# Attention scores from 64-row products on the two partition halves, without stacked copies

## What is computed

```
q = l2norm(x Wq) * q_scale            # (8 batches, 16 heads, 512, 64)
k = l2norm(x Wk) * k_scale
v = x Wv
attn = softmax(q k^T * 64**-0.5)      # 512 x 512 for each head
out  = (attn v) Wo + bo
x    = x + gate_a * out
x    = x + gate_b * moe(layernorm(x) * (1 + cb) + sb)
```

## Time and profile of the kernel before

| | |
|---|---|
| median of 3 runs | 1470.58 us (1469.07 to 1471.44) |
| span of the profiled execution | 1467.0 us |
| attention stage | from about 45 us to 1131 us |
| PE busy over the span | 1343.3 us (92%) |
| DVE, ACT, POOL busy over the span | 1103.4, 1058.0, 645.9 us |
| SBUF-to-SBUF copies into `stack` | 256 DMAs of 384 KB, 6.4 us from issue to landing |

### The profile page before, as it was taken

The page is one execution under the profiler, slowest core; times in us unless marked ns, Lnnn a source line. Parts: engine busy times, 40 slices in busy tenths (PEclk is TensorE's granted clock), DMA queues, the critical chain, the costliest instruction groups (busy, mean ns, idle before and its releaser), DMA issues. The chain is left out here.

```text
span 1467.0 us, 27427 instructions
## 1 busy us (share of the span) xinstructions
PE 1343.3 (92%) x7114; PEld 913.1 (62%) x7114; DVE 1103.4 (75%) x2179; ACT 1058.0 (72%) x2650; POOL 645.9 (44%) x1279
## 2 busy tenths in 40 slices
PE   4699999999999999999999999999998377899997
PEld 4566666666665666666566666666654255677775
DVE  4478768776886787688768876876874798588887
ACT  3577868876887687688768877876875366677776
POOL 2245435543534454344336433443433666344443
PEclk8799999999999999999999999999999599899999
DMA  5344334543334344333435433354334000534331
GB/s 126 87 106 111 87 87 93 120 95 85 89 88 99 80 111 106 88 87 87 98 82 113 100 90 87 87 118 100 86 87 115 1 0 0 119 88 98 89 91 39
DMA packets 90054, 129.05 MB, mean 88 GB/s; under 512 B 12816, under 2 KB 55320, under 8 KB 89880
## 3 DMA queue, kind: packets, MB, share of 16 engines
q1 hardware_dynamic: 88696, 126.67, 38.3%
q10 hardware_dynamic: 1184, 0.40, 0.1%
HBM read 24.16 MB, written 2.23 MB: 18 GB/s over the span
## 5 line engine op out<-in xcount | busy, mean ns | idle before, releaser
L814 DVE TENSOR_REDUCE neg_max<-bank 128x1 f32<-128x512 f32 x512 | 350.2, 684 | 219.1 <-PE bank L525 212.5
L687 ACT ACTIVATE probs<-bank,neg_max 128x512 f32<-128x512 f32 x512 | 354.1, 692 | 144.1 <-DVE neg_max L814 139.5
L534 PEld LDWEIGHTS bank<-ident,probs 128*128 128x128 f32 x2048 | 236.1, 141 | 243.2 <-issue 150.0
L534 PE MATMUL bank<-ident,probs 128*128 128x128 f32 x2048 | 322.7, 280 | 1.9 <-ACT probsT L695 1.9
L556 PE MATMUL bank<-probsT,v_tok 128*64 128x512 f32 x1024 | 275.7, 617 | 0.9 <-DVE probsT L821 0.9
L524 PE MATMUL bank<-operands 128*128 128x512 f32 x512 | 236.8, 462 | 30.9 <-DMA operands<-operands 14.6
L50 POOL TENSOR_TENSOR rn_t<-rn 128x16 f32<-128x16 f32 x192 | 43.0, 224 | 367.5 <-DVE rn L41 357.5
L525 PE MATMUL bank<-operands 128*128 128x512 f32 x512 | 203.9, 398 | 0.0
L821 DVE COPY probsT<-bank 128x512 f32<-128x512 f32 x256 | 173.7, 678 | 0.6 <-PE bank L534 0.6
L661 ACT ACTIVATE qk_tok<-bank 128x256 f32<-128x256 f32 x256 | 99.1, 387 | 97.2 <-PE bank L494 96.8
L695 ACT ACTIVATE probsT<-bank 128x512 f32<-128x512 f32 x256 | 153.6, 600 | 11.3
(11 more groups left out here) (214 smaller groups left out, 2609.0 us busy)
## 6 DMA issues: line engine op xcount, KB each, us to landing
operands<-operands SPq DMA_DIRECT2D x256, 384.0 KB, 6.4
probsT<-gate_scratch SPq DMA_DIRECT2D x64, 256.0 KB, 5.0
out<-x_all SPq DMA_DIRECT2D x8, 256.0 KB, 2.4
probsT<-in_L_ffn_fc_w SPq DMA_DIRECT2D x1, 1024.0 KB, 8.9
raw<-in_L_attn_Wq SPq DMA_DIRECT2D x1, 512.0 KB, 4.6
raw<-in_L_attn_Wk SPq DMA_DIRECT2D x1, 512.0 KB, 7.5
raw<-in_L_attn_Wv SPq DMA_DIRECT2D x1, 512.0 KB, 8.8
raw_o<-in_L_attn_Wo SPq DMA_DIRECT2D x1, 512.0 KB, 8.9
```

What stands on the lines that cost most here:

```text
L534: last = nc.tensor.transpose(T_BANK[i % 2][:, j * P:(j + 1) * P], probs[:, i % 4, j * P:(j + 1) * P], ident[:])
L687: nc.scalar.activation(probs[:, i % 4], S_BANK[i % 3][:], ACT.Exp, bias=neg_max[:, i:i + 1], accum_out=row_sum[:, hp % 2, i:i + 1]).then_i ...
L814: nc.vector.reduce_max(neg_max[:, i:i + 1], S_BANK[i % 3][:], AX.X, negate=True).then_inc(max_done, 1)
```

## The change

`stack`, the four DMAs and the semaphores `stack_a` and `stack_b` are gone. `parts` is kept twice, for even and odd units, in the same SBUF space. `scores` makes a pair of tiles at once, the same 128 queries of both heads. It issues six products of 64 rows, head 0's on partitions 0 to 63 and head 1's on 64 to 127, in turns, into two PSUM banks. So `slot` calls it at even steps only. A tile's number i now means token tile i // 2 and head i % 2, and the banks rotate over a whole batch (`s_bank`). `high_q`, which writes the parts of the next unit, waits for the score products of the unit that used the same half of `parts`, instead of for the DMAs.

```
-    def scores(u, hp, i):
-        g = S_TILES * u + i
-        if i == 0:
-            pe.wait_ge(stack_a, 32 * (u + 1))
-        if i == NT:
-            pe.wait_ge(stack_b, 32 * (u + 1))
-        after(pe, p_done, g - (2 if i >= 3 else 4 if i == 2 else 1))
-        head, t = i // NT, i % NT
-        st = stack[:, hp % 2, head]
-        q = st[:, ST_Q, t * P:(t + 1) * P]
-        nc.tensor.matmul(S_BANK[i % 3][:], q, st[:, ST_K], start=True, stop=False)
-        nc.tensor.matmul(S_BANK[i % 3][:], q, st[:, ST_KX], start=False, stop=True).then_inc(s_ready, 1)
+    def scores(u, hp, pair):
+        if pair == 0:
+            pe.wait_ge(kl_done, u + 1)
+        first = S_TILES * hp + 2 * pair
+        after(pe, p_done, S_TILES * u + 2 * pair + (0 if first == 0 else -1))
+        toks = slice(pair * P, (pair + 1) * P)
+        own = parts[:, hp % 2]
+        for q, k in ((QH, KH), (QH, KL), (QL, KH)):
+            for head in range(2):
+                rows = slice(head * DH, (head + 1) * DH)
+                last = nc.tensor.matmul(s_bank(hp, 2 * pair + head)[:], own[rows, q, toks], own[rows, k],
+                                        start=((q, k) == (QH, KH)), stop=(q == QL))
+                if q == QL:
+                    last.then_inc(s_ready, 1)
...
     for i in range(S_TILES):
-        if main:
-            scores(u, hp, i)
+        if main and i % 2 == 0:
+            scores(u, hp, i // 2)
...
+    def s_bank(hp, i):
+        return S_BANK[(S_TILES * hp + i) % 3]
...
     def high_q(u, hp):
         act.wait_ge(qt_ready, u + 1)
-        after(act, stack_a, 32 * u)
-        after(act, stack_b, 32 * u)
+        after(act, s_ready, S_TILES * (u - 1))
...
-    def stacks(u, hp):                     
-        sp.wait_ge(kl_done, u + 1)
-        for head in range(2):
-            own, other = (0, DH) if head == 0 else (DH, 0)
-            src = parts[own:own + DH]
-            dst = stack[:, hp % 2, head]
-            there = (stack_a, stack_b)[head]
-            sp.dma_start(dst[own:own + DH].bitcast(F32), src[:, QH:QL:-1].bitcast(F32)).then_inc(there, 16)
-            sp.dma_start(dst[other:other + DH].bitcast(F32), src[:, QL:QH].bitcast(F32)).then_inc(there, 16)
```

More of the change, by code:

```diff
@@ L28 @@
 QL, KL, KH, QH = range(4)
-ST_Q, ST_K, ST_KX = range(3)
 def after(engine, semaphore, value):
@@ L106, in adaln_attention_moe @@
         operands = sb("operands", [P, 16 * N], F32R)
-        stack = operands[:, 0:12 * N].rearrange("p (a h s n) -> p a h s n", a=2, h=2, s=3)
-        parts = operands[:, 12 * N:].rearrange("p (k n) -> p k n", k=4)
+        parts = operands[:, 0:8 * N].rearrange("p (a k n) -> p a k n", a=2, k=4)
         h2_h, h2_l = operands[:, 0:T], operands[:, T:2 * T]
@@ L395, in adaln_attention_moe @@
             kl_done = sem("kl_done")
-            stack_a = sem("stack_a")
-            stack_b = sem("stack_b")
             s_ready = sem("s_ready")
@@ L671, in high_q, with high_k @@
                         act.wait_ge(qt_ready, u + 1)
-                        after(act, stack_a, 32 * u)
-                        after(act, stack_b, 32 * u)
-                        nc.scalar.activation(parts[:, QH], XT_BANK[:], ACT.Copy,
+                        after(act, s_ready, S_TILES * (u - 1))
+                        nc.scalar.activation(parts[:, hp % 2, QH], XT_BANK[:], ACT.Copy,
                                              scale=qk_scale[:, hp % HP:hp % HP + 1]).then_inc(qh_done, 1)
-                    def high_k(u):
+                    def high_k(u, hp):
                         act.wait_ge(kt_ready, u + 1)
-                        nc.scalar.activation(parts[:, KH], XT_BANK[:], ACT.Copy).then_inc(kh_done, 1)
+                        nc.scalar.activation(parts[:, hp % 2, KH], XT_BANK[:], ACT.Copy).then_inc(kh_done, 1)
                     def exponentials(u, hp, i):
@@ L686, in exponentials @@
                             after(act, inv_done, u - 1)
-                        nc.scalar.activation(probs[:, i % 4], S_BANK[i % 3][:], ACT.Exp, bias=neg_max[:, i:i + 1],
+                        nc.scalar.activation(probs[:, i % 4], s_bank(hp, i)[:], ACT.Exp, bias=neg_max[:, i:i + 1],
                                              accum_out=row_sum[:, hp % 2, i:i + 1]).then_inc(p_done, 1)
@@ L693, in copy_transposed @@
                             after(act, av_done, u - 1)
-                        head, t = i // NT, i % NT
+                        t, head = i // 2, i % 2
                         nc.scalar.activation(probsT[:, hp % 2, head, :, t * P:(t + 1) * P],
@@ L738, in slot @@
                             if front_b and i == KT_AT + 1:
-                                high_k(u + 1)
+                                high_k(u + 1, hp + 1)
                             if not is_const(b, LAST) and (hp, i) == (H1T_AT[0], H1T_AT[1] + 1) and main:
@@ L764, in _ @@
                     high_q(0, 0)
-                    high_k(0)
+                    high_k(0, 0)
                     over_batches(act, batch)
@@ L801, in low_q, with low_k, row_max @@
                         dve.wait_ge(qh_done, u + 1)
-                        nc.vector.scalar_tensor_tensor(out=parts[:, QL], in0=XT_BANK[:],
+                        nc.vector.scalar_tensor_tensor(out=parts[:, hp % 2, QL], in0=XT_BANK[:],
                                                        scalar=qk_scale[:, hp % HP:hp % HP + 1],
-                                                       in1=parts[:, QH].bitcast(F32), op0=ALU.mult,
+                                                       in1=parts[:, hp % 2, QH].bitcast(F32), op0=ALU.mult,
                                                        op1=ALU.subtract).then_inc(ql_done, 1)
-                    def low_k(u):
+                    def low_k(u, hp):
                         dve.wait_ge(kh_done, u + 1)
-                        nc.vector.tensor_tensor(parts[:, KL], XT_BANK[:], parts[:, KH].bitcast(F32),
+                        nc.vector.tensor_tensor(parts[:, hp % 2, KL], XT_BANK[:], parts[:, hp % 2, KH].bitcast(F32),
                                                 ALU.subtract).then_inc(kl_done, 1)
-                    def row_max(u, i):
+                    def row_max(u, hp, i):
                         dve.wait_ge(s_ready, S_TILES * u + i + 1)
-                        nc.vector.reduce_max(neg_max[:, i:i + 1], S_BANK[i % 3][:], AX.X, negate=True).then_inc(max_done, 1)
+                        nc.vector.reduce_max(neg_max[:, i:i + 1], s_bank(hp, i)[:], AX.X, negate=True).then_inc(max_done, 1)
                     def copy_transposed(u, hp, i):
@@ L879, in slot @@
                             if main:
-                                row_max(u, i)
+                                row_max(u, hp, i)
                             if tail and i < P_LAG:
@@ L889, in slot @@
                             if front_b and i == KT_AT + 1:
-                                low_k(u + 1)
+                                low_k(u + 1, hp + 1)
                             if front_a and i in (3, 4):
@@ L942, in _ @@
                     low_q(0, 0)
-                    low_k(0)
+                    low_k(0, 0)
                     dve.wait_ge(x_in, 16)
@@ L970, in widen @@
                         after(pool, r_ready, u)
-                        src = inv_sum[:, hp % 2].rearrange("p (h t) -> p t h", h=2)
+                        src = inv_sum[:, hp % 2].rearrange("p (t h) -> p t h", h=2)
                         nc.gpsimd.tensor_tensor(inv_wide[:], src.unsqueeze(3).to_broadcast([P, NT, 2, DH]),
```

## The result

The changed kernel takes 1489.9 us (median of 4, 1488.7 to 1490.8) where the kernel before takes 1470.5. The ratio is 1.0131, with a 95% interval of 1.0116 to 1.0145: 19.4 us slower. The forecast was slower by 41, so the direction was right, and the measured change is less than half of the forecast one.

What follows compares the result with a forecast made beforehand. The prediction took PE to bound the attention stage. Its terms, 14 + 48 - 6 - 15 + 2 = +43 us on the span of 1467.0, gave 1510 us, taken as 1512 us for the median, range 1452 to 1572.

Steps and rivals of the forecast that it cites:

- order: waits of projections 1 and 3, less the covered ones: PE's projections 1 and 3 wait for ACT's copy out of the one bank: +48 us, less 6 us covered by other work.
- row halves: Six 64-row score products per pair, with borders entering and leaving the halves: +0.22 us for each unit, +14 us.
- copies gone, first pair of a batch: SP's DMA waits vanish, -15 us; each batch's first pair waits for the previous batch's last exponentials, +2 us.
- What bounds the kernel: PE bounds the attention stage: a unit of 15.53 us is the sum of PE's pieces plus its waits.
- Part 2: Projections 1 and 3 lose the score tile between them and their predecessors: +0.77 us in 62 units, +48, less 6 covered.
- The walk: Step through one unit: exponentials of tile 0, which release scores 2 and 3, have 0.2 us of cover; no further wait.
- Part 1: Score products of the two heads run side by side, three steps of 0.23 us plus borders per pair: +14 us.
- A: Rival: the row halves don't run side by side, so a pair takes six steps: +179, 1691 us; chance 0.12.
- the 0.2 us of cover: Time by which PE reaches scores 2 and 3, likewise 4 and 5, after the exponentials they need could release them.
- Part 3: SP's four DMAs per unit go with their 14.6 us of waits, -15 us; loop-border "issue", 14.2 us, stays; first pairs +2.
- B: Rival: cheap row-half borders make the kernel faster, 1430 us at the lower bound, mostly near 1455; chance 0.20.
- C: Rival: filling two of three banks at once makes score pairs wait for exponentials, some 25 us more: 1540; chance 0.08.

Runs made afterwards that it cites:

- pairs_only: The kernel before, with its 128-row products and copies, but tiles i and i+1 issued together at even steps: ratio 1.0350, 51 us slower.
- full_array: The changed kernel with four 128-row products for a pair of tiles in place of six 64-row ones: ratio 1.0113, 1486.3 us.
- tq_first: The changed kernel with transpose_q moved ahead of project at step 1, into the gap between projections 0 and 1: ratio 1.0124, 1489.4 us.
- one_half: The changed kernel with both heads' products on partitions 0 to 63, head 0's computed twice: ratio 1.1296, 1662 us.
- copies_idle: The changed kernel with the four copies of each unit back on SP, into unused space, PE waiting for none: ratio 1.0270, 1508.2 us.
- copies_off_border: The changed kernel with the old copies back on SP into unused space, except those of each batch's first unit: ratio 1.0149, 1491.0 us.
- covered: The changed kernel with transpose_q and transpose_k ahead of projections 1 and 3, ACT's exponentials before its square, DVE's low_q before copy_transposed: 1.0197, 1500.4 us.
- interleaved: The changed kernel with projections laid between pairs and transposes on PE, high_q and squares later on ACT, low_q earlier on DVE: 1.0213, 1498.9 us.

## Why the prediction missed

By its own parts, with the runs that measured each:

| term | forecast, us | measured, us | from |
|---|---|---|---|
| order: waits of projections 1 and 3, less the covered ones | +42 | +42 | pairs_only, +51.5, less 14.3 at its loop ends, plus 4.5 of DMA waits |
| row halves | +14 | +3 (-1 to +6) | changed less full_array |
| copies gone, first pair of a batch | -13 | -25 | full_array less pairs_only, -35, plus the same 14.3, less 4.5 |
| sum | +43 | +19 | |

The three measured terms must add up to the whole, since they are steps of one chain of runs. That the first is 42 and the third 25 rests on the loop ends and DMA waits of single profiled executions. The traces of before and after give nearly the same third term: the first score product is 6.1 us sooner, the other DMA waits (7.3 us) are gone, and the loop ends add 12.4 us less, 26 in all, of which new waits at the batches' first pairs that the loop ends don't hold give back 2 to 3.

- **What bounds the kernel.** Right. Distances of ends priced PE's pieces to 0.02 us: 0.91 for 0.89, 1.43 for 1.45.
- **Part 2, the order.** Right in mechanism, place and size. The unit lengthened by 0.75 us in pairs_only (15.53 to 16.28), and 0.77 was forecast. In the changed kernel it is 0.85, that is 0.77 of waits and 0.10 for the row halves, within 0.02. The walk also had the next bound right: with the projection's wait covered, tq_first found the exponentials there.
- **Part 1, side by side.** Right, and A was wrong: one_half shows what A would have cost. The size was off by 11 us. The step that failed is the sum of the borders over four pairs: for pair 0 the 0.13 was 0.11, but at pair 1 full-array work would have waited 0.06 for the exponentials, so half of its border was free, and pairs 2 and 3 gained 0.05 each instead of 0.02. The prediction knew of the 0.2 us of cover and did not use it on this term.
- **Part 3, what goes away.** This is where it failed: "The loop borders ('issue', 14.2 us) stay." They went, and the slower clock behind them too: the loop ends added 19.0 us before and add 6.6 after. "Issue" had been read as PE's own cost of a loop, because it named no releaser, and the copies had been priced by the waits that name them. copies_idle and copies_off_border show that the waits were the copies' doing, by traffic and not by data. The first pairs of the batches cost more than the 2 us forecast: PE waits 4.0 us there for exponentials, and 8.4 in all places. With the 14.2 us of "issue" in its sum the prediction would have said +29, and with 3 for the row halves in place of 14 it would have said +18.
- **B and C.** Neither was the cause: a pair with both borders cost 1.04 (0.89 + 0.15), where B needed less than 0.89, and PE's waits for exponentials in the changed kernel are 8.4 us in 15 places, where C needed 25 more.

## What to carry to other kernels

When steps of a hand-written order are merged, list for every single-buffered hand-over what lay between its two ends, and recompute that distance: here one score tile of 0.47 us had been the cover of a copy, and moving it by one step cost 42 us, more than any other part of the change. Cover one wait and look for the next in the other engine's list, in order; moving work on PE without moving what releases it (covered, interleaved) made things worse twice. And an idle time without a releaser isn't a constant of the engine: look at what the DMA engines do in that stretch, and at the granted clock behind it, before leaving it in the sum.

## What the runs showed of the hardware

- Four SBUF-to-SBUF copies of 384 KB in flight when PE's loop branches lengthen that branch from 3.3 to 3.8 us to 4.9 to 6.5 us (five loop ends each in four kernels). The branch ends 1.3 to 2.4 us after a 16 KB packet of instructions has landed, and the copies delay that packet's start by about 1 to 3 us. Two such packets at once lengthen the branch to 5.1 us without copies and to 7.1 to 7.9 us with them. The same copies elsewhere cost nothing measurable (56 units, 1.0149 for 1.0131).
- Behind such a loop end the granted clock was 0.50 for 3.4 or 6.8 us in 11 of 15 cases with copies and in none of 15 without. In the kernel before, 3.4 us of it cost about 1.2 us.
- Two streams of 64-row float32r products on the two row halves take one step of 0.23 us for two products; both on one half take two steps. Entering the halves from full-array work cost 0.20 us (0.89 for a pair, less three steps of 0.23), and leaving them 0.15, the same as for column halves. Where `weigh_values` on the column halves follows a pair, only its own entry of 0.15 us is paid between the two (1.01 us for the group, as before).
